# Two-layer network on one Trainium2 core: first feed-forward network with low-rank products in two passes from stacked operands, and gate and up in eleven tiles, the last shared by both

## The reference

```python
B, L, D = (2, 128, 256)
E, TOP_K, RANK, DFF = (8, 2, 8, 688)
def _lora(x, A, Bm, scale):
    return x @ A @ Bm * scale
def _expert_lora(x, A, Bm, w, scale):
    xA = jnp.einsum('bld,edr->bler', x, A)
    xAB = jnp.einsum('bler,erd->bled', xA, Bm) * scale
    return (xAB * w).sum(axis=2)
```

## Time and profile before

| | |
|---|---|
| median of 3 runs | 1401.04 us (1400.85 to 1401.22) |
| the profiled execution, its own time | 1409.79 us |
| its span in the profile | 1408.0 us |
| TensorE matmuls | 1350.0 us busy (96%) |
| TensorE weight loads | 1108.4 us (79%) |
| DVE | 993.7 us (71%) |
| ACT | 611.3 us (43%) |
| POOL | 566.9 us (40%) |

### The profile page before, as it was taken

The page is one execution under the profiler, slowest core; times in us unless marked ns, Lnnn a source line. Parts: engine busy times, 40 slices in busy tenths (PEclk is TensorE's granted clock), DMA queues, the critical chain, the costliest instruction groups (busy, mean ns, idle before and its releaser), DMA issues.

```text
span 1408.0 us, 24791 instructions
## 1 busy us (share of the span) xinstructions
PE 1350.0 (96%) x8292; PEld 1108.4 (79%) x8292; DVE 993.7 (71%) x2519; ACT 611.3 (43%) x1497; POOL 566.9 (40%) x466
## 2 busy tenths in 40 slices
PE   8999999999999999899999999999999999985995
PEld 7788888888888888788887888888888888863664
DVE  5788888888888888865454565765765666874226
ACT  4555555555555555642323333433433434441332
POOL 3776656565656565802104232222222212313222
PEclk9999999999999999999999999999999999987998
DMA  6000000000000200120000200200200002777994
GB/s 190 1 12 1 13 0 11 0 11 0 11 0 11 66 0 1 21 70 1 0 1 0 76 8 16 76 9 16 75 8 15 8 9 53 203 260 227 282 266 135
DMA packets 67952, 76.16 MB, mean 54 GB/s; under 512 B 14189, under 2 KB 55173, under 8 KB 67877
## 3 DMA queue, kind: packets, MB, share of 16 engines
q1 hardware_dynamic: 56533, 58.36, 14.3%
q10 hardware_dynamic: 8560, 12.36, 3.0%
q0 software_dynamic: 2784, 4.46, 1.6%
HBM read 66.22 MB, written 8.95 MB: 53 GB/s over the span
## 4 chain that ended last, share of the span: by engine, by line
PE 83%; DVE 6%; ACT 4%; issue 3%; DMA 2%; another core or an unknown queue 1%; POOL 0%; SPq 0%; DVEq 0%; ACTq 0%; POOLq 0%
PE ps L1857 43%; PE ps L2003 9%; PE ps L1958 6%; PE ps L2040 4%; PE ps L1964 2%; PE ps L2225 2%; PE ps L1978 2%; PE ps L1974 2%; PE ps L1975 2%; DMA wo<-in_L_attn_wo_dram 1%; PE ps L2215 1%; PE ps L2452 1%; PE ps L2138 1%; PE ps L2374 1%; PE ps L2139 1%
## 5 line engine op out<-in xcount | busy, mean ns | idle before, releaser
L860 ACT ACTIVATE probs<-ps,nm 128x128 f32<-128x128 f32 (+3 forms) x256 | 135.4, 529 | 198.7 <-DVE nm L1277 198.7
L717 POOL TENSOR_TENSOR qk<-q,ksb 128x512 f32<-128x512 f32 x64 | 85.7, 1340 | 306.2 <-ACT q L978 214.6
L2003 PE MATMUL ps<-kT,qT 128*128 128x128 f32 (+3 forms) x512 | 159.3, 434 | 3.2 <-ACT probs L860 3.2
L1209 DVE TENSOR_TENSOR prod<-ps,rope_sb 128x1024 f32<-128x1024 f32 x128 | 155.5, 1217 | 7.3 <-PE ps L1857 7.3
L557 POOL TENSOR_TENSOR qT<-prod 64x512 f32<-64x512 f32 x64 | 82.0, 1281 | 140.5 <-DVE prod L1209 133.3
L1187 DVE TENSOR_TENSOR pT_low<-ps,pT 128x384 fp32r<-128x384 f32 (+2 forms) x256 | 104.8, 451 | 44.4 <-ACT pT L794 44.4
L1277 DVE CUSTOM_DVE_ANT_0 ps<-ps,causal 128x128 f32<-128x128 f32 (+3 forms) x256 | 122.7, 500 | 3.1 <-PE ps L2003 3.0
L557 POOL TENSOR_TENSOR kT<-prod 64x512 f32<-64x512 f32 x64 | 82.1, 1282 | 70.2 <-DVE prod L1209 64.8
L1857 PEld LDWEIGHTS ps<-kvo,qn 128*128 128x128 f32 x768 | 100.8, 192 | 8.6 <-DVE qn L1187 3.9
L1331 DVE SCALAR_TENSOR_TENSOR acc<-ps,rinv,acc 128x256 f32<-128x256 f32 x256 | 106.0, 476 | 2.1 <-issue 2.1
L794 ACT ACTIVATE pT<-ps 128x384 fp32r<-128x384 f32 (+2 forms) x256 | 84.9, 415 | 51.4 <-PE ps L2040 51.3
(11 more groups left out here) (303 smaller groups left out, 3046.9 us busy)
## 6 DMA issues: line engine op xcount, KB each, us to landing
eg<-in_L_ffn_w_gate_dram SPq DMA_DIRECT2D x16, 704.0 KB
eg<-in_L_ffn_w_up_dram SPq DMA_DIRECT2D x16, 704.0 KB
ed<-in_L_ffn_w_down_dram ACTq DMA_DIRECT2D x10, 640.0 KB
ksb<-ks_dram SPq DMA_DIRECT2D x16, 256.0 KB, 3.3
ed<-in_L_ffn_w_down_dram SPq DMA_DIRECT2D x6, 640.0 KB
rows_dram<-rows ACTq DMA_DIRECT2D x4, 640.0 KB, 7.7
acc<-in_L_attn_x_dram SPq DMA_DIRECT2D x4, 512.0 KB
wq_in<-in_L_attn_wq_dram SPq DMA_DIRECT2D x8, 256.0 KB, 2.9
```

Source lines behind the costliest of these rows:

```text
L717: nc.gpsimd.tensor_tensor(qk[:], q3[:], ksb[b % 2][:], ALU.mult).then_inc(qk_ready, 1)
L860: nc.scalar.activation(probs[hh][:, off:off + (i + 1) * P], ps[:, BS + i % 2, 0:(i + 1) * P], ACT.Exp, bias=nm[:, hh, i:i + 1], scale=-1.0 ...
L1209: nc.vector.tensor_tensor(prod[parity][w][:], ps[:, BA:BA + 2, :], rope[:, w:w + 1, :].broadcast_to([P, 2, T]), ALU.mult).then_inc(product ...
L2003: pe.matmul(ps[:, bank, 0:(i + 1) * P], qT[:, hh, b, i * P:(i + 1) * P], kT[:, hh, b, 0:(i + 1) * P], start=True, stop=True).then_inc(scor ...
```

## The change

**Low-rank products.** Instead of three products with 72 inner rows, each low-rank part takes two products with more inner rows. `lb_wide` holds the high half of `lb`'s first 64 rows twice, in partitions 0 to 63 and 64 to 127; `xaT_wide` holds the high half of `xaT`'s first 64 rows above and their low half below. So one product of 128 inner rows does high by high and high by low. `lb_rest` has 104 rows: the low half of rows 0 to 63, the low half of rows 64 to 71, and the high half of rows 64 to 71 again; `xaT_rest` has the high half of all 72 rows, rows 64 to 71 again, 16 rows of zeros and the low half of rows 64 to 71. The doubled rows come from the source: SP loads `B`'s last expert four more times for each column range, and DVE's routing writes the last expert's `xa` a second time, so that 80 columns a side are turned.

**Tiles.** The 688 features are cut into 4 tiles of 128, one of 112 and one of 64. In tile 5, 64 gate columns and 64 up columns stand side by side in `gu`, so six products make both, into one PSUM bank, gate in its partitions 0 to 63 and up in 64 to 127. `lb` has 64 columns of zeros between the two, so that its gate and up products can add into the same bank.

**What moves with it.** ACT makes the lower rows of `lb_wide` after the last of POOL's halvings, and two copies per side of `xaT` instead of one; DVE makes two rests per side. POOL has three more instructions for `lb` and two clearings. The waits on counts follow.

```diff
-F0S = [(i * 115, 115) for i in range(4)] + [(460, 114), (574, 114)]
+F0S = [(i * 128, 128) for i in range(4)] + [(512, 112), (624, 64)]
...
-        w0_pieces.append(([h[:] for h in lb], lb_in[:]))
+        w0_pieces.append(([lb_wide[0:64], lb_rest[0:64]], lb_in[0:64]))
...
             def load_small():
                 for w, name in enumerate(("gate", "up")):
-                    sp.dma_start(lb_in[0:R0, w, :], io["L0_ffn_sB_" + name]).then_inc(lb_loaded, 16)
-                    sp.dma_start(lb_in[R0:NL, w, :], io["L0_ffn_B_" + name].rearrange("e r n -> (e r) n")).then_inc(lb_loaded, 16)
+                    for to, lo, hi in ((0, 0, F0),) if w == 0 else ((F0 + size, f, F0), (F0 + 2 * size, 0, f)):
+                        cols = slice(to, to + hi - lo)
+                        sp.dma_start(lb_in[0:R0, cols], io["L0_ffn_sB_" + name][:, lo:hi]).then_inc(lb_loaded, 16)
+                        sp.dma_start(lb_in[R0:NL, cols],
+                                     io["L0_ffn_B_" + name][:, :, lo:hi].rearrange("e r n -> (e r) n")).then_inc(lb_loaded, 16)
+                        for at in range(NL, NB, R0):
+                            sp.dma_start(lb_in[at:at + R0, cols], io["L0_ffn_B_" + name][E0 - 1][:, lo:hi]).then_inc(lb_loaded, 16)
...
+
+            one = ones[64:NB, :].broadcast_to([NB - 64, LB])
+            nc.gpsimd.tensor_tensor(lb_rest[64:NB], lb_in[64:NB], one, ALU.mult).then_inc(w0_hi, 1)
+            nc.gpsimd.memset(xaT_rest[64:96].bitcast(F32), 0.0)
+            pool.wait_ge(w0_hi, w0_first + 1 + 7)
             pool.wait_ge(w0_lo, w0_first + 6)
+            nc.gpsimd.tensor_tensor(lb_rest[64:NL], lb_in[64:NL], lb_rest[64:NL].bitcast(F32), ALU.subtract).then_inc(w0_lo, 1)
+            pool.wait_ge(w0_lo, w0_first + 7)
...
                 for w in range(2):
                     act.wait_ge(xa_turned, b * 2 + (w + 1))
-                    copy(xaT[0][:, w, :], ps[0:NL, xa_bank(b) + w, :]).then_inc(xahi_ready, 1)
+                    copy(xaT_wide[0:64, w, :], ps[0:64, xa_bank(b) + w, :])
+                    copy(xaT_rest[0:NX, w, :], ps[0:NX, xa_bank(b) + w, :]).then_inc(xahi_ready, 1)
...
+
+            act.wait_ge(w0_lo, w0_first + 7)
+            copy(lb_wide[64:P], lb_in[0:64])
             xa_halves(0)
...
                     dve.wait_ge(xahi_ready, b * 2 + (w + 1))
-                    rest(xaT[1][:, w, :], ps[0:NL, xa_bank(b) + w, :], xaT[0][:, w, :]).then_inc(xalo_ready, 1)
+                    rest(xaT_wide[64:P, w, :], ps[0:64, xa_bank(b) + w, :], xaT_rest[0:64, w, :])
+                    rest(xaT_rest[96:NB, w, :], ps[64:NL, xa_bank(b) + w, :], xaT_rest[64:NL, w, :]).then_inc(xalo_ready, 1)
...
                 f, size = F0S[m]
+                if m == FT0 - 1:
+                    for k in range(KD):
+                        mm3(ps[:, m % 2, :], lambda a: gu[a][:, k, f:f + 2 * size], lambda c: x1T[b % 2][c][:, k, :], k == 0, False)
+                    return
...
-                    last = mm3(ps[0:size, 2 * w + m % 2, :], lambda a: lb[a][:, w, f:f + size],
-                               lambda c: xaT[c][:, w, :], False, True)
+                    at, wide, bank = f + w * (F0 + 2 * F0S[-1][1]), size, 2 * w + m % 2
+                    if m == FT0 - 1:
+                        at, wide, bank = f + w * size, 2 * size, m % 2
+                    pe.matmul(ps[0:wide, bank, :], lb_wide[:, at:at + wide], xaT_wide[:, w, :], start=False, stop=False)
+                    last = pe.matmul(ps[0:wide, bank, :], lb_rest[:, at:at + wide], xaT_rest[:, w, :], start=False,
+                                     stop=w == 1 or m < FT0 - 1)
...
-            pe.wait_ge(w0_lo, w0_first + 6)
+            pe.wait_ge(w0_lo, w0_first + 7)
```

More of the change, by code:

```diff
@@ L119, in program @@
         oT_low = place("oT_low", 197, [P, T], F32R)
-        gu_in = place("gu_in", 89, [P, KD, 2, F0])
-        lb_in = place("lb_in", 137, [NL, 2, F0])
+        gu_in = place("gu_in", 89, [P, KD, 2 * F0])
+        lb_in = place("lb_in", 137, [NB, LB])
         dn = place("dn", 174, [M0, FT0, D + NL])
@@ L128, in program @@
         ldn = place("ldn", 140, [NL, D])
-        gu = [place(f"gu{h}", 20 + 11 * h, [P, KD, 2, F0], F32R) for h in range(2)]
-        lb = [place(f"lb{h}", 42 + 5.5 * h, [NL, 2, F0], F32R) for h in range(2)]
-        la = [place(f"la{h}", 53 + 1.25 * h, [P, KD, NA], F32R) for h in range(2)]
+        gu = [place(f"gu{h}", 20 + 11 * h, [P, KD, 2 * F0], F32R) for h in range(2)]
+        lb_wide = place("lb_wide", 42, [P, LB], F32R)
+        lb_rest = place("lb_rest", 47.625, [NB, LB], F32R)
+        la = [place(f"la{h}", 53.25 + 1.25 * h, [P, KD, NA], F32R) for h in range(2)]
         x1T = [[place(f"x1T{i}{h}", at + 4 * h, [P, KD, T], F32R) for h in range(2)] for i, at in enumerate((60, 102))]
-        xaT = [place(f"xaT{h}", 56 + 12 * h, [NL, 2, T], F32R) for h in range(2)]
+        xaT_wide = place("xaT_wide", 68, [P, 2, T], F32R)
+        xaT_rest = place("xaT_rest", 56, [NB, 2, T], F32R)
         gated = [place(f"gated{h}", 72 + 2 * h, [M0, T]) for h in range(2)]
@@ L139, in program @@
         haT = place("haT", 88, [NL, T])
-        xa = place("xa", 90, [P, TPB, 2 * NL])
+        xa = place("xa", 90, [P, TPB, 2 * NX])
         ha = place("ha", 92.5, [P, TPB, NL])
@@ L363, in wait_gathered @@
                 engine.wait_ge(gathered[q], 16 * (GROUPS // 4))
-        w0_pieces = [([h[:, k, w, :] for h in gu], gu_in[:, k, w, :]) for w in (1, 0) for k in range(KD)]
+        w0_pieces = [([h[:, k, F0 * w:F0 * w + F0] for h in gu], gu_in[:, k, F0 * w:F0 * w + F0]) for w in (1, 0) for k in range(KD)]
         w0_pieces.insert(2, ([h[:] for h in la], la_in[:]))
-        w0_pieces.append(([h[:] for h in lb], lb_in[:]))
+        w0_pieces.append(([lb_wide[0:64], lb_rest[0:64]], lb_in[0:64]))
         def x1_bank(b):
@@ L419, in load_small @@
                                      io["L0_ffn_A_" + name].rearrange("e (k p) r -> k p e r", p=P)[k]).then_inc(la_loaded, 16)
-            for lo, hi, size in ((0, 4, 115), (4, 6, 114)):
+            for lo, hi, size in ((0, 4, 128), (4, 5, 112), (5, 6, 64)):
                 inner = slice(F0S[lo][0], F0S[hi - 1][0] + size)
@@ L615, in _ @@
             pool.wait_ge(roped, 4 * PROJECTIONS)
-            pool.wait_ge(gu_loaded, 32)
+            pool.wait_ge(gu_loaded, 48)
+            nc.gpsimd.memset(lb_in[:, F0:F0 + F0S[-1][1]], 0.0).then_inc(w0_hi, 1)
             for m, (halves, whole) in enumerate(w0_pieces):
@@ L939, in dn_halves @@
                     copy(dn_high[1][:, 0:1, :], dn[:, 3:4, :])
-                    copy(dn_high[1][0:114, 1:3, :], dn[0:114, 4:6, :]).then_inc(dn_hi, 1)
+                    copy(dn_high[1][0:112, 1:2, :], dn[0:112, 4:5, :])
+                    copy(dn_high[1][0:64, 2:3, :], dn[0:64, 5:6, :]).then_inc(dn_hi, 1)
             def ffn0(b, last):
@@ L947, in ffn0 @@
                         act.wait_ge(hid_ready, b * FT0 + (m - 1))
-                    nc.scalar.activation(gated[m % 2][0:size, :], ps[0:size, m % 2, :], ACT.Silu).then_inc(gated_ready, 1)
+                    o = gated[m % 2][0:size, :] if m < FT0 - 1 else gated[m % 2][64:64 + size, :]
+                    nc.scalar.activation(o, ps[0:size, m % 2, :], ACT.Silu).then_inc(gated_ready, 1)
                     act.wait_ge(hid_ready, b * FT0 + (m + 1))
@@ L1390, in route0 @@
                 settle()
+                for k in range(2):
+                    nc.vector.tensor_tensor(
+                        xa[:, 2 * k:2 * k + 2, :].rearrange("p i (w c) -> p i w c", w=2)[:, :, :, NL:NX],
+                        ps[:, bank + k, 0:2 * NA].rearrange("p (i c) -> p i c", i=2)[:, :, E0:NA].rearrange(
+                            "p i (w c) -> p i w c", w=2)[:, :, :, NL - R0:NL],
+                        wnext[:, 2 * k:2 * k + 2, E0:E0 + 1].rearrange("p i (a e) -> p i a e", a=1).broadcast_to([P, 2, 2, R0]),
+                        ALU.mult)
                 for i in range(TPB):
@@ L2113, in ffn0 @@
                         pe.wait_ge(hid_ready, b * FT0 + (m - 1))
-                        for w in range(2):
+                        for w in range(2 if m < FT0 - 1 else 1):
                             base(m, w)
```

47 lines of the change are left out of this document (29 added, 18 removed).

## The result

The changed kernel takes 1416.34 us (median of 4 runs, 1415.07 to 1417.83), the kernel before, beside it, 1400.94: ratio 1.0116, 95% interval 1.0103 to 1.0129. It is slower by 15.4 us, where 2.9 were forecast.

The account below looks back on a forecast made before the run. TensorE was taken to bound the first network, except at batch heads and the network's start; 8.1 us at the start plus 5.3 between batches less 10.5 saved gave +2.9, 1403.9 us, range 1398.5 to 1407.5.

Parts of the forecast that it names:

- What the change removes: Prediction's passage on TensorE products saved per batch in the first network; 128 instead of 115 stationary columns cost nothing.
- Saved, 10.5 us: Fewer TensorE products in the first network: 2.4 us in each of batches 0 to 2, 3.3 in the last.
- The 4.0 us from tile 4 to the logits: TensorE's interval from tile 4's end to the first logits product shrinks from 5.03 to 4.0 us, giving 1.0.
- the new wait of 0.69 us for `x1T`: Before the logits products, TensorE newly waits at least 0.6 us for DVE to end `x1T`'s low half.
- Between batches, 5.3 us: At three transitions, DVE's four rests delay the `acc` additions and TensorE's tile 2 by 1.75 us each; 5.3 us lost.
- the chain that the prediction named: Between batches, late `acc` additions delay statistics, POOL's root, normalization and first Silu, so tile 2 starts 1.75 us later.
- Rival 2: Late start with clock fall, plus one to three falls between batches, 1.6 us each: +4.5 to +7.7 us; chance 0.25.
- The start, 8.1 us: At the network's start, late `la` and longer POOL `lb` work delay tile 2: 8.1 us with clock fall, 6.5 without.
- POOL's full price for 40 and 8 rows: In POOL's `lb` work, few-row ops cost like full ones, so it ends at 613.9; at nothing, 608.0.
- Rival 5: Start hidden because SP's 14 extra issues cost little; only -5.2 us stays, 1395.8 us; chance 0.12.
- The sum: Whole kernel: 8.1 us at the start plus 5.3 between batches less 10.5 saved, +2.9 us.
- The carry-over to the median: Whole kernel: the unchanged kernel's median lies 8.75 us below its profiled execution; this difference was carried over, giving 1403.9.

Follow-up runs that it names:

- tile 5 stacked: Changed kernel with tile 5's down products taking rounded hidden rows and their remainder as one 128-row operand, two products instead of three; ratio 1.0013 to the kernel before.
- the first of the mends together: Changed kernel with that stacked tile 5, `la_in`'s transfers issued ahead of `lb_in`'s and the `xaT_rest` memset early; ratio 0.9972 to the kernel before.

## Why the prediction was wrong

- **The step that failed: the terms of the sum left the down products out.** "What the change removes" asks what 128 stationary columns cost and says nothing of the contraction rows, which fall to 64 in tile 5. They cost 12.2 us by the trace; undone alone they give 10.6 to 13.0 us back (15.4 and 17.8 less the 4.8 of that run), done alone they cost 11.1. Without them the kernel would have come out 3 to 6 us over before, inside the range; that this lies near the forecast is partly luck, as the next points show.
- **Saved, 10.5 us:** right, 10.1. The 4.0 us from tile 4 to the logits and the new wait of 0.69 us for `x1T` came as worked out.
- **Between batches, 5.3 us:** the mechanism was right, the size was not: 3 x 2.56 = 7.7. The additions came 2.11 us later and not 1.75 (four rests take 2.84 us, not twice 1.21), and the chain that the prediction named, through root, normalization and Silu, passed this on whole. Rival 2's fall of the clock came, but in the base products and not in tile 2, and it cost 0.45 us each time and not 1.6. Two later runs (tile 5 stacked, and the first of the mends together) show this at their third transition, where the clock did not fall: tile 2 came 13.54 us behind `ldn`, 2.12 more than before. TensorE in the stacked run there:

```profile
746.05 5.85 PE L1902 MATMUL ps<-x1T,gu 128*128 128x512 f32 x24 [2.27 <-DVE acc L1522]
...
755.34 3.06 PE L1902 MATMUL ps<-x1T,gu 128*128 128x512 f32 x12 [1.51 <-DVE hidT L1483]
```

- **The start, 8.1 us:** 9.5, of which 1.7 are the chance fall of the clock at 588, so 7.8. POOL's full price for 40 and 8 rows was right. SP's 8-row issues took 0.37 us, so `la` came at 591.47 and not 593.4; POOL's wait alone would have cost less (by the trace gate's base products could have started at 611.74 and not at 616.01). That VectorE's routing is held by POOL's instructions, so that TensorE's long wait is for `xa`, was in no case: the close number is luck. (The terms of this path also add up to 622.7 and not 622.9.)
- **Rival 5** (the start hidden) fell. The 14 extra issues put the last of `la_in` 5.23 us later (582.30 to 587.53), 0.37 each, and `la` 6.1 us later.
- **The sum:** 9.5 + 7.7 + 12.2 - 10.1 = 19.3 us, the network's 19.4. At the last products of the second layer's shared expert 19.2 are left (1290.44 against 1271.27). Behind them before waits 2.00 us for VectorE and then the 8.48 us, after 0.74 in all. The medians differ by 15.4 and 17.8. What their executions waited there no trace shows, so where the last two to four went stays open; the kernel before alone spreads by 2.9 us (1398.29 to 1401.22).
- **The carry-over to the median:** taking 8.75 us off was right for before, but it was for the most part one wait in another stage, which the trace could have shown. The profiled execution of after has no such wait and lies 1.2 us over its median.

## What to carry to other kernels

When tile sizes change, list every product that takes the tile, as its stationary columns and as its contraction rows, and keep sizes over 64 or stack two halves to 128 (sizes under 64 were not run). A wait that ends on one engine is often the middle of a chain over three: before an instruction is moved up, name what waits at the chain's end, and what is queued behind the moved one on each engine. Keep long GpSimd work off the moments in which VectorE does short operations in SBUF on the way to TensorE.
